# Self attention on TensorE: both score blocks' products drawn up behind the products of the first maxima, and the unit's sum moved one step back

## The reference

```python
def sdpa(q, k, v, causal):
    scale = 1.0 / np.sqrt(q.shape[-1])
    scores = jnp.einsum('bhqd,bhkd->bhqk', q * scale, k)
    if causal:
        mask = jnp.tril(jnp.ones((q.shape[-2], k.shape[-2]), dtype=bool))
        scores = jnp.where(mask, scores, jnp.finfo(jnp.float32).min)
    p = jax.nn.softmax(scores.astype(jnp.float32), axis=-1).astype(q.dtype)
    return jnp.einsum('bhqk,bhkd->bhqd', p, v)
```

## Time and profile before

| | us |
|---|---|
| median of 3 runs | 3631.37 |
| lowest and highest run | 3630.75, 3647.57 |
| span of the profiled execution | 3628.6 |
| self attention in it, first maxima product to last output | 157 to 324 |
| busy over the span: PE, DVE, ACT, POOL | 3390.8, 2019.1, 1846.1, 1589.9 |

### The profile page before, as it was taken

One profiled execution on the slowest core, in us unless ns is written; L12 is line 12 of the kernel. 1 busy time (PEld: TensorE's weight loads), 2 busy tenths in 40 slices (PEclk: granted clock), 3 DMA queues, 4 the chain that ended last, 5 costly groups with the idle time before them and its releaser, 6 DMA issues. The chain is left out here.

```text
span 3628.6 us, 74082 instructions
## 1 busy us (share of the span) xinstructions
PE 3390.8 (93%) x25048; PEld 2305.3 (64%) x25048; DVE 2019.1 (56%) x3324; ACT 1846.1 (51%) x3374; POOL 1589.9 (44%) x1421
## 2 busy tenths in 40 slices
PE   7798799898999799989999999999999998999997
PEld 5556544344444388866666666666666666878886
DVE  4465577776777454435555555555555553114454
ACT  2254277676776533335555555555555553333333
POOL 3213012221221011107777777777777775005554
PEclk9899799999999899999999999999999999999998
DMA  4784200000000222220000000000001003220200
GB/s 120 170 131 120 79 7 18 17 17 17 17 18 27 96 74 100 107 112 10 13 31 14 32 13 32 16 30 15 33 29 42 13 13 119 82 75 1 98 7 12
DMA packets 74751, 179.36 MB, mean 49 GB/s; under 512 B 14720, under 2 KB 44928, under 8 KB 68480
## 3 DMA queue, kind: packets, MB, share of 16 engines
q1 hardware_dynamic: 70240, 161.81, 14.7%
q0 software_dynamic: 4128, 12.60, 1.3%
HBM read 115.09 MB, written 59.26 MB: 48 GB/s over the span
## 5 line engine op out<-in xcount | busy, mean ns | idle before, releaser
L1654 POOL TENSOR_TENSOR cross_acc<-cross_acc,cross_probs 128x512 f32<-128x512 f32 (+1 forms) x704 | 921.4, 1309 | 159.9 <-ACT cross_probs L1717 118.6
L1717 ACT ACTIVATE cross_probs<-cross_s,cross_bias 128x512 f32<-128x512 f32 (+1 forms) x832 | 530.3, 685 | 488.9 <-PE cross_s L1936 487.1
L1813 DVE TENSOR_REDUCE cross_partmax<-cross_r 128x1 f32<-128x400 f32 (+1 forms) x1024 | 541.2, 570 | 334.3 <-PE cross_r L1906 316.0
L1256 DVE TENSOR_REDUCE cross_partmax<-cross_m 128x2 f32<-128x800 f32 (+1 forms) x512 | 497.0, 991 | 187.1 <-PE cross_m L1359 186.1
L1167 ACT ACTIVATE cross_probs<-cross_s 128x512 f32<-128x512 f32 (+1 forms) x832 | 453.9, 596 | 150.7 <-PE cross_s L1379 150.4
L1949 PE MATMUL cross_av<-cross_probs,cross_v 128*64 128x256 f32 (+1 forms) x3328 | 459.1, 394 | 0.0
L1949 PEld LDWEIGHTS cross_av<-cross_probs,cross_v 128*64 128x64 f32 (+1 forms) x3328 | 199.5, 136 | 173.2 <-ACT cross_probs L1717 77.3
L1106 POOL TENSOR_TENSOR cross_diag<-c_ident,cross_negmax 128x256 fp32r<-128x256 f32 x128 | 76.0, 615 | 497.6 <-DVE cross_negmax L1264 497.6
L1390 PE MATMUL cross_av<-cross_probs,cross_v 128*32 128x256 f32 (+1 forms) x3328 | 269.0, 395 | 10.2 <-ACT cross_probs L1167 9.0
L1802 DVE TENSOR_TENSOR cross_k_lo<-cross_r,cross_k_hi 128x400 fp32r<-128x400 f32 (+1 forms) x256 | 146.4, 572 | 192.4 <-ACT cross_k_hi L1695 192.4
L1930 PE MATMUL cross_s<-cross_q_hi,cross_k_hi 64*128 64x256 f32 (+1 forms) x1664 | 253.0, 299 | 0.0
(11 more groups left out here) (307 smaller groups left out, 6479.6 us busy)
## 6 DMA issues: line engine op xcount, KB each, us to landing
d_masked_ctx<-tail_ctx_split SPq DMA_DIRECT2D x8, 1602.0 KB, 5.3
d_self_qk<-selfproj_qk_split POOLq DMA_DIRECT2D x32, 256.0 KB, 5.5
self_qs<-d_self_qk SPq DMA_DIRECT2D x64, 128.0 KB, 8.0
self_ks<-d_self_qk SPq DMA_DIRECT2D x64, 128.0 KB, 8.5
d_cross<-tail_pr SPq DMA_DIRECT2D x8, 1024.0 KB, 4.6
cross_qp<-d_cross SPq DMA_DIRECT2D x64, 128.0 KB, 2.4
d_cross<-cross_out SPq DMA_DIRECT2D x64, 128.0 KB, 1.8
tail_attn<-d_cross SPq DMA_DIRECT2D x8, 1024.0 KB, 5.5
```

The source lines that it names most:

```text
L1256: nc.vector.tensor_reduce(partmax[:, :, jt // 2, jt % 2, i:i + 1], m_pair(sets[q], w), AX.X, ALU.max).then_inc(maxed, 1)
L1654: nc.gpsimd.tensor_tensor(acc[0:w, g % 2], left, probs[0:w, slot % NPB], ALU.add).then_inc(added, 1)
L1717: nc.scalar.activation(probs[0:w, (g * KT + t) % NPB], src_, ACT.Exp, scale=XHD ** -0.5, bias=bias[0:w, p, t:t + 1]).then_inc(probs_ready, 1)
L1813: nc.vector.tensor_reduce(partmax[:, m, i:i + 1], r_ps[MAX_BANK[q]][:, 0:KCH[i][1]], AX.X, ALU.max).then_inc(maxed, 1)
```

## The change

PE's step becomes: products of the first maxima of unit n + 2; products of both score blocks of n + 1; the masks of those maxima; masks and shifts of both blocks; sums of unit n - 1; values of n; second maxima of n + 2 (products and masks). To that end maxima is cut into max_products and max_masks, scores into score_products, which waits for the exponentials, and score_shifts, which waits for the diagonals (block 0). ScalarE's step becomes: exponentials of n + 1; logarithm and inverse of n - 1; copy of n. The last step does its own sum too. SyncE, GpSimd and VectorE keep their lists, and no operation, size or buffer is changed.

```diff
--- before.py
+++ after.py
@@ -438,6 +438,12 @@
     return None if isinstance(b, int) and b == B - 1 else (b + 1, 1 - p, 0, n + 1)
 
 
+def preceding(u, per):
+
+    n = u[3] - 1
+    return n // per, n // per % 2, n % per, n
+
+
 def self_attention(nc, c, ph, early, ahead_, out_d):
 
 
@@ -526,18 +532,28 @@
                     nc.scalar.activation(p1[:, g % 2].rearrange("p (i k) s -> p i (k s)", i=2), two_banks(s1_ps, 2 * P), ACT.Exp,
                                          scale=SHD ** -0.5).then_inc(p1_ready, 1)
 
-                def step(u, nxt):
+                def copy_av(u):
                     b, p, g, n = u
                     act.wait_ge(av_ready, n + 1 + PRIME)
                     act.wait_ge(out_ready, n - 1 + PRIME)
                     nc.scalar.activation(av[:, g % 2], av_ps[:, 0:S], ACT.Copy).then_inc(av_copied, 1)
-                    if nxt:
-                        exponentials(nxt)
+
+                def inverse_sum(u):
+                    b, p, g, n = u
                     act.wait_ge(sum_ready, n + 1 + PRIME)
                     nc.scalar.activation(ln_sum[:], sum_ps[:, 0:S], ACT.Ln).then_inc(ln_ready, 1)
                     act.wait_ge(ln_ready, n + 1 + PRIME)
                     act.wait_ge(out_ready, n + PRIME)
                     nc.scalar.activation(rsum[:], ln_sum[:], ACT.Exp, scale=-1.0).then_inc(rsum_ready, 1)
+
+                def step(u, nxt):
+                    if nxt:
+                        exponentials(nxt)
+                    if u[3]:
+                        inverse_sum(preceding(u, NG))
+                    copy_av(u)
+                    if not nxt:
+                        inverse_sum(u)
 
                 each_unit(NG, exponentials, step)
 
@@ -575,7 +591,7 @@
             def _(pe):
                 prime(pe, max_ready, s0_ready, s1_ready, av_ready, sum_ready)
 
-                def maxima(u, jj):
+                def max_products(u, jj):
 
                     b, p, g, n = u
                     if b == 0 and jj == 0:
@@ -588,24 +604,33 @@
                         for i in range(2):
                             nc.tensor.matmul(max_ps[i][:, t * P:t * P + (t + 1) * P], qs[ROWS[i], b % 3, pair, t * P:(t + 1) * P],
                                              ks[ROWS[i], b % 3, pair, 0:(t + 1) * P], start=(t == 0), stop=False)
+
+                def max_masks():
                     for i in range(2):
                         o = max_ps[i][:].rearrange("p (t s) -> p t s", t=2)[:, :, 0:P]
                         nc.tensor.matmul(o, c["ident_b"][:], c["causal"][:, 0, 0:P].unsqueeze(1).to_broadcast([P, 2, P]),
                                          start=False, stop=True).then_inc(max_ready, 1)
 
-                def scores(u, t):
+                def maxima(u, jj):
+                    max_products(u, jj)
+                    max_masks()
+
+                def score_products(u, t):
+                    b, p, g, n = u
+                    lo, w = t * P, S - t * P
+                    ps = (s0_ps, s1_ps)[t]
+                    pe.wait_ge((p0_ready, p1_ready)[t], n + PRIME)
+                    for jj in range(2):
+                        for i in range(2):
+                            nc.tensor.matmul(ps[:, i * 512 + jj * w:i * 512 + (jj + 1) * w], ks[ROWS[i], b % 3, 2 * g + jj, lo:lo + P],
+                                             qs[ROWS[i], b % 3, 2 * g + jj, lo:S], start=(jj == 0), stop=False)
+
+                def score_shifts(u, t):
                     b, p, g, n = u
                     lo, w = t * P, S - t * P
                     ps = (s0_ps, s1_ps)[t]
                     if t == 0:
                         pe.wait_ge(diag_ready, n + 1 + PRIME)
-                        pe.wait_ge(p0_ready, n + PRIME)
-                    else:
-                        pe.wait_ge(p1_ready, n + PRIME)
-                    for jj in range(2):
-                        for i in range(2):
-                            nc.tensor.matmul(ps[:, i * 512 + jj * w:i * 512 + (jj + 1) * w], ks[ROWS[i], b % 3, 2 * g + jj, lo:lo + P],
-                                             qs[ROWS[i], b % 3, 2 * g + jj, lo:S], start=(jj == 0), stop=False)
                     for i in range(2):
                         o = ps[:, i * 512:i * 512 + 2 * w].rearrange("p (j s) -> p j s", j=2)
                         nc.tensor.matmul(o[:, :, 0:P], c["ident_b"][:], c["causal_tb"][:, 0, 0:P].unsqueeze(1).to_broadcast([P, 2, P]),
@@ -639,22 +664,31 @@
                     for w in (u, following(u, NG)):
                         maxima(w, 0)
                         maxima(w, 1)
-                    scores(u, 0)
-                    scores(u, 1)
+                    for t in range(2):
+                        score_products(u, t)
+                    for t in range(2):
+                        score_shifts(u, t)
 
                 def step(u, nxt):
                     after = nxt and following(nxt, NG)
                     if after:
-                        maxima(after, 0)
+                        max_products(after, 0)
+                    if nxt:
+                        for t in range(2):
+                            score_products(nxt, t)
+                    if after:
+                        max_masks()
+                    if nxt:
+                        for t in range(2):
+                            score_shifts(nxt, t)
+                    if u[3]:
+                        sums(preceding(u, NG))
                     values(u, 0)
                     values(u, 1)
-                    if nxt:
-                        scores(nxt, 0)
                     if after:
                         maxima(after, 1)
-                    if nxt:
-                        scores(nxt, 1)
-                    sums(u)
+                    if not nxt:
+                        sums(u)
 
                 each_unit(NG, ahead, step)
```

## The result

| | before | after |
|---|---|---|
| median of the runs, us | 3634.71 (4 runs) | 3666.22 (4 runs, 3663.53 to 3670.87) |
| ratio | | 1.0081, 95% interval 1.0060 to 1.0103 |
| span of the profiled execution, us | 3628.6 | 3661.7 |
| first maxima product to last sum product, us | 156.96 to 321.39: 164.4 | 156.46 to 356.37: 199.9 |
| 29 steps, by the masks of the second maxima, us | 172.26 to 314.56: 142.3 | 172.11 to 347.99: 175.9 |

The kernel became slower by 0.8%. The profiled executions differ by 33.1 us. The stage takes 35.5 us more, but its first product came 0.5 us earlier and what follows its last sum product took 1.9 us less (3305.3 against 3307.2 us), so the whole difference lies in self attention.

What follows compares the result with a forecast made beforehand. PE's order of issue in self attention bounds the step, 4.91 us. 29 steps at 5.80 add 25.8 us, last steps 1.9 and step 0 0.1: 27.8 on the median 3631.4 gives 3659.2 us, range 3650 to 3672 (80%).

Steps and rivals of the forecast that it cites:

- the widening: The forecast's own range, 3654 to 3664 us, stretched to 3650 and 3672 for later stages' clock changes and part of the first rival.
- signs of being wrong: In the changed trace: a step under 5.5 us, PE idle for ScalarE or a load, or half a clock in steady steps.
- run of products: First maxima and both score blocks on PE, six pairs in a row: about 0.84 us instead of 1.22.
- entry of 0.09 us: PE's extra time on changing into products with 64 active rows, seen behind block 0's shifts; two such entries a step go.
- bank wait: Next first maxima wait until VectorE's reductions free the shared banks: 1.40 us from masks, PE pausing about 1.07 us a step.
- diagonals' wait: PE waits before block 0's shifts for VectorE's diagonals: up to 0.37 us more, 2.85 us after the second maxima's masks.
- the ring: PE and VectorE close each step together: 2.94 us of PE work plus 2.85 us back to the shifts, taken as 5.80.
- second rival: Only the bank wait counts, diagonals ready in time: step 5.42 us, 17 us more in sum, 3648 us; chance 6%.
- first rival: PE's clock falls in the pauses: 3724 us if it lasts, 3681 us for a third of the steps; chance 10%.
- The ends: The stage's last steps take 1.9 us more (bounds 0 to 3), step 0 takes 0.1 us more (bounds -0.5 and 0.5).
- cover of the later loads: Query and key loads on SyncE come about 4 us later against the step; 5.3 us more before their use covers it.
- moved sum: Preceding unit's sum placed ahead of the values, ScalarE's list reordered: no cost, ScalarE needing under 3 us of 5.8.

Runs made afterwards that it cites:

- e7_both_blocks: Kernel before with score block 1's products drawn up directly behind block 0's; typical step 4.77 us against 4.91, whole time 3630.49 us in one run.
- e1_fill: Changed kernel plus nine useless mask matmuls on TensorE behind the second maxima; every step 5.80 us, 29 steps 168.2 us against 175.9, whole time 3668.73 us.
- e2_split: Changed kernel with the diagonals made in two half-size instructions, each with its own signal; typical step 5.51 us against 5.80, whole time 3653.92 us.
- e5_last: Kernel before with only the second maxima moved to the end of the step; typical step 5.99 us against 4.91, whole time 3676.82 us.
- e6_sum: Kernel before with the preceding unit's sum ahead of the values and ScalarE's list reordered to match; typical step 5.45 us against 4.91, whole time 3655.24 us.
- e11_sum_order: e6_sum with ScalarE's logarithm and inverse of the preceding unit ahead of the exponentials; typical step 5.04 us against 5.45, whole time 3649.89 us.
- e3_early: Changed kernel with the second maxima moved to right behind the score shifts, ahead of sum and values; typical step 4.58 us, ratio to kernel before 0.9985.
- e9_half_loads: e3_early without the loads of keys from batch 3 on; all 29 steps 4.58 us, 132.8 us against 139.5, whole time 3639.47 us.
- e4_early_split: e3_early with the diagonals made in two half-size instructions; typical step 4.94 us against 4.58, ratio to kernel before 0.9984.

## Why the prediction was right

3666.22 us lie in the range of 3650 to 3672, and the sign was forecast with 89%. The waits were forecast by place and size. That the number lies inside is in part the doing of the widening: the forecast's own bounds, 3654 to 3664, don't hold it, and one of its signs of being wrong, half a clock in steady steps, appeared in five of 29. Some of the distance from 3659 is scatter, too: the median of the kernel before rose from 3631.37 to 3634.71 us with a fourth run. By its steps:

- **What the run of products gives.** Forecast 0.84 us for six pairs, measured 0.84 or 0.85. The entry of 0.09 us behind block 0's shifts went as forecast: the two halves take 182.24 to 182.95, 0.71 us, instead of 0.36 + 0.45. e7_both_blocks shows the shorter run with four pairs.
- **The bank wait.** Forecast 1.40 us from masks to products; measured 1.39 or 1.40 in most steps and 1.48 or 1.49 in others, in seven kernels (after, e1_fill, e2_split, e5_last, e6_sum, e7_both_blocks, e11_sum_order). Where the 0.09 comes from was not followed. Its source was the stage's own first maxima.
- **The diagonals' wait and the ring.** Forecast up to 0.37 us, 2.85 us from masks to shifts and a step of 5.80; measured 0.38 where the bank distance is 1.39 and 0.28 where it is 1.48, 2.85 and 5.80. e2_split took this wait away alone and the step fell to 5.51; the forecast's second rival, 5.42 with this wait absent, was about the right size for that kernel, and wrong for the change.
- **The clock.** Here a term is missing from the sum. The first rival (10%: the clock falls in the pauses) came true in part: not for a third of the steps, but for five of 29, 7.7 us. The argument against it, 17.70 us busy of 20 at full clock in another stage, was too weak for a step with PE busy for about 15 to 16 us of 20. e1_fill shows the cause. Without it the forecast of 27.8 us would have stood against 33.1 - 7.7 = 25.4 us.
- **The ends.** Forecast 1.9 us, measured 1.5. Step 0 was forecast at 0.1 us and came out at 0.3: 156.46 to 172.11 is 15.65 us, before it was 15.30.
- **The cover of the later loads.** It held: no wait for a load. It held because the step grew, as the text said; in e3_early, with the same later issue and a step of 4.58 us, loads do jam, and e9_half_loads shows that half of them don't.
- **The moved sum "at nothing".** The step of 5.80 us leaves no room for a cost of it in the changed order, but the reason is one the text didn't give: the waits are open there anyway. In the order of before it costs 0.13 us a step at best (e11_sum_order), since it is part of what hides the bank wait.

## What to carry to other kernels

Work between two users of the same buffer is cover: before drawing like instructions together, measure the distance that the other engine needs (here 1.39 us from masks to a free bank, 2.85 us to the diagonals) and count what the new order leaves in it. The place of one group decided 1.22 us a step here (5.80 against 4.58 in e3_early), and the gain of 0.37 us a step from longer runs was lost in it; with the second maxima ahead of the sum and the values both fit. And when a step gets shorter, look for the next limit in advance: the busy share of the DMA engines, 0.89, was in the profile of the kernel before. Look at the average as well as the typical step: in e3_early they are 4.81 and 4.58 us.

## What the runs showed of the hardware beyond that

- TensorE's granted clock swings with two pauses, 1.45 us together, in each step of 5.80 us: five stretches at 1.2 GHz in 176 us, mean clock 0.95, 7.7 us lost. With one pause of 1.07 to 1.17 us in 5.51 us (e2_split) or in 6 us (e5_last) no step of that kind was seen, in one execution of each, and nine useless matmuls in the longer pause of the changed kernel end it.
- VectorE's product of two SBUF operands and GpSimd's don't run beside each other at full pace, and it is the one that starts later that stretches. In e4_early_split GpSimd's, started 0.20 us behind VectorE's first half, takes 1.08 us instead of 0.73, and VectorE's second half, which meets it, up to 1.22 instead of 0.69. In e3_early VectorE's long product starts 0.20 us ahead and keeps its 1.22 us in all 32 units, and GpSimd's takes 1.62:

```profile
214.86 1.22 DVE L575 TENSOR_TENSOR self_diag<-c_ident,self_negmax 128x1024 fp32r<-128x1024 f32 x1
...
215.06 1.62 POOL L516 TENSOR_TENSOR self_out<-self_av,self_rsum 128x256 f32<-128x256 f32 x1 [2.96 <-ACT self_rsum L547]
```

- Ends of matmuls are modelled, so a wait of 0.2 us shows in most steps as no idle time of PE (e7_both_blocks, e11_sum_order). The distance between starts, compared with the other engine's release, finds it.
